# The last expert's rows: added on chip and written to the output, instead of added in device memory before a final copy

## What is computed

```python
logits = xt @ wg
gates_k, idx_k = top_k(softmax(logits), 2)          # 2 of 8 experts per token
gates_k = gates_k / sum(gates_k)
disp[e, slot] = xt[token]                            # 8 x 1024 slots, 256 features
h   = relu(einsum('ecd,edh->ech', disp, w1) + b1)    # 256 -> 1024
out = einsum('ech,ehd->ecd', h, w2) + b2             # 1024 -> 256
y   = sum over the token's two experts of gate * out[expert, slot]
x   = x + tanh(g_ffn[1]) * y
```

## Time and profile before

| | us |
|---|---|
| runs shown (three) | 2085.93, 2087.16, 2091.36 |
| their median | 2087.16 |
| the profiled execution, its own time | 2089.91 |
| the profiled execution, its span | 2088.2 |
| last matmul of the program ends | 2065.36 |
| last add issued (start) | 2069.08 |
| copy to the output issued | 2072.80 |
| copy, from issue to landing | 15.0 |

### The profile page before, as it was taken

How to read it: one execution, slowest core, us unless ns; L and a number is a source line. 1 busy time by engine, 2 the same in 40 slices (tenths; PEclk the granted TensorE clock), 3 DMA queues, 4 the chain that set the end, 5 groups by cost and what they waited for, 6 DMA issues and landing times. The chain is left out here.

```text
span 2088.2 us, 29804 instructions
## 1 busy us (share of the span) xinstructions
PE 1779.8 (85%) x10491; PEld 1063.2 (51%) x10491; DVE 1070.1 (51%) x2740; ACT 888.4 (43%) x1684; POOL 605.0 (29%) x580
## 2 busy tenths in 40 slices
PE   3799898989864988737999999999954999999995
PEld 1456555555544877613344444443322666666664
DVE  4556877787745644306877777778321112121121
ACT  3366565655531222222777787766721111111110
POOL 4212211120002777622221233211132233333322
PEclk9999999999976999967999999999976999999998
DMA  3545445334224778625323432431114133333314
GB/s 114 167 121 173 151 137 169 107 121 134 75 74 117 172 164 171 114 75 164 102 67 114 132 119 77 126 110 58 42 47 132 30 78 81 81 76 76 81 20 101
DMA packets 204243, 222.84 MB, mean 107 GB/s; under 512 B 33438, under 2 KB 195231, under 8 KB 203431
## 3 DMA queue, kind: packets, MB, share of 16 engines
q1 hardware_dynamic: 176458, 177.48, 27.7%
q0 software_dynamic: 27648, 43.60, 11.1%
HBM read 155.06 MB, written 86.93 MB: 116 GB/s over the span
## 5 line engine op out<-in xcount | busy, mean ns | idle before, releaser
L889 DVE TENSOR_REDUCE nmx<-mxb 128x1 f32<-128x512 f32 (+1 forms) x896 | 521.7, 608 | 244.0 <-PE mxb L660 147.8
L747 ACT ACTIVATE pt<-stb 128x512 f32<-128x512 f32 x832 | 475.3, 598 | 280.5 <-PE stb L680 155.9
L660 PE MATMUL mxb<-kst,qst 96*128 96x512 bf16 (+4 forms) x1024 | 335.9, 350 | 36.9 <-DVE nmx L889 27.2
L677 PE MATMUL stb<-qst,kst 99*128 99x512 bf16 (+4 forms) x1024 | 327.6, 345 | 8.2 <-DMA qst<-m3T 4.3
L1569 PE MATMUL e_h_bank<-e_xT,e_w 128*128 128x512 f32 x512 | 224.7, 597 | 6.1 <-ACT e_xT L1609 5.4
L1583 PE MATMUL e_y_bank<-e_w,e_h 128*128 128x256 f32 x1024 | 227.0, 379 | 0.0
L693 PE MATMUL ob<-pt,va 128*32 128x512 f32 (+3 forms) x2048 | 220.3, 525 | 2.7 <-ACT pt L747 1.7
L1583 PEld LDWEIGHTS e_y_bank<-e_w,e_h 128*128 128x128 f32 x1024 | 193.0, 190 | 31.7 <-issue 7.2
L677 PEld LDWEIGHTS stb<-qst,kst 102*128 102x128 bf16 (+1 forms) x1024 | 99.5, 99 | 213.3 <-ACT pt L747 136.0
L1171 POOL TENSOR_TENSOR qk<-qk,parts 128x512 f32<-128x512 f32 x64 | 73.0, 1161 | 436.4 <-ACT qk L782 227.8
L1723 POOL DMA_INDIRECT x_after_l<-e_y,e_token x64 | 99.5, 1555 | 282.0 <-DVE e_y L1688 267.3
(11 more groups left out here) (242 smaller groups left out, 2514.7 us busy)
## 6 DMA issues: line engine op xcount, KB each, us to landing
qk_parts<-parts SPq DMA_DIRECT2D x16, 1536.0 KB, 6.2
qst<-qk_parts SPq DMA_DIRECT2D x384, 64.0 KB, 2.3
kst<-qk_parts SPq DMA_DIRECT2D x384, 64.0 KB, 2.3
e_w<-in_L_ffn_w SPq DMA_DIRECT2D x16, 1024.0 KB, 7.4
rows<-rows SPq DMA_DIRECT2D x15, 1060.0 KB, 8.7
crow<-in_ctx SPq DMA_DIRECT2D x16, 512.0 KB, 3.9
x_after_l<-xres SPq DMA_DIRECT2D x16, 512.0 KB, 3.3
e_gu_nat<-in_L_ffn_gate_up_proj SPq DMA_DIRECT2D x64, 128.0 KB
```

Of the source, the lines that this page charges most:

```text
L660: last = pe.matmul(out, qst[par][0:rows_used, h, qt * P:(qt + 1) * P], kst[par][0:rows_used, h, 0:nk], start=True, stop=not causal)
L677: last = pe.matmul(bank[:, to:to + S - q_from(kt)], kst[par][0:ROWS, h, kt * P:(kt + 1) * P], qst[par][0:ROWS, h, q_from(kt):S], start=Tru ...
L747: act.activation(pt[:, slot(b, u), q0:S], stb[no % N_ST][:, q0:S], ACT.Exp, scale=SCALE).then_inc(s["st_free"], 1)
L889: last = dve.tensor_reduce(nmx[:, qt, h:h + 1], got[:, at:at + k_to(qt)], AX.X, ALU.max, negate=True)
```

## The change

The last expert does not add in device memory any more. Once the adds of experts 0 to 6 have landed, two things are issued: SP copies the sum as it then stands to the output, and POOL gathers from the same sum the rows of the last expert's tokens into a new buffer `sums` (`e_sums`). DVE waits for these rows ahead of emptying the first bank of expert 7, and for that expert multiplies by the gate and adds the gathered row in one instruction (`scalar_tensor_tensor`). POOL then waits for the copy and writes each finished tile over its tokens' rows in the output, by an indirect DMA without accumulation; rows of empty slots lie past the end and are dropped. SP and POOL end by waiting for these writes.

```diff
@@ sync
             pipeline(sp, E1, first, iteration)
-            sp.wait_ge(s["added"], 16 * TILES * E1)
+            sp.wait_ge(s["added"], 16 * TILES * (E1 - 1))
             sp.dma_start(out, x[0:T, :]).then_inc(s["copied"], 16)
             sp.wait_ge(s["copied"], 16)
+            sp.wait_ge(s["written"], 16 * TILES)
@@ vector
-            def result(b, blk):
+            def result(b, blk, last=False):
...
                 if blk == 0:
                     dve.wait_ge(s["picked"], at(2, b, 2))
+                    if last:
+                        dve.wait_ge(s["sum_in"], 16 * TILES)
...
                     for i in (2 * trip, 2 * trip + 1):
-                        dve.tensor_scalar(y[par][:, i, :], y[par][:, i, :], wcol[par][:, i:i + 1], None, ALU.mult).then_inc(s["y_done"], 1)
+                        if last:
+                            dve.scalar_tensor_tensor(out=y[par][:, i, :], in0=y[par][:, i, :], scalar=wcol[par][:, i:i + 1],
+                                                     in1=sums[:, i, :], op0=ALU.mult, op1=ALU.add).then_inc(s["y_done"], 1)
+                        else:
+                            dve.tensor_scalar(y[par][:, i, :], y[par][:, i, :], wcol[par][:, i:i + 1], None, ALU.mult).then_inc(s["y_done"], 1)
@@ gpsimd
+            def gather_sums(b):
+                pool.wait_ge(s["picked"], at(2, b, 2))
+                pool.wait_ge(s["added"], 16 * TILES * (E1 - 1))
+                for i in range(TILES):
+                    pool.indirect_dma_start(sums[:, i, :], None, x, bass.IndirectOffsetOnAxis(token[b[1]][:, i:i + 1], 0),
+                                            bounds_check=T + SPARE - 1, oob_is_err=True).then_inc(s["sum_in"], 16)
+
+            def write(b):
+                pool.wait_ge(s["copied"], 16)
+                for i in range(TILES):
+                    pool.wait_ge(s["y_done"], at(TILES, b, i + 1))
+                    pool.indirect_dma_start(out, bass.IndirectOffsetOnAxis(token[b[1]][:, i:i + 1], 0), y[b[1]][:, i, :], None,
+                                            bounds_check=T - 1, oob_is_err=False).then_inc(s["written"], 16)
+
             def iteration(cur, nxt):
                 if nxt:
                     gather(nxt)
-                add(cur)
+                    add(cur)
+                else:
+                    gather_sums(cur)
+                    write(cur)
```

More of the change, by code:

```diff
@@ L1499, in experts1 @@
                  "h_full", "act_h", "dve_h", "y_full", "y_evac", "y_done", "added", "picked", "small", "ichain",
-                 "copied", "passed")
+                 "copied", "passed", "written", "sum_in")
         s = {n: ctx.enter_context(nc.semaphore(f"e1_{n}")) for n in names}
@@ L1507, in experts1 @@
         y = two("y", [P, TILES, D])
+        sums = t_("sums", [P, TILES, D])
         b1_s, b2_s = t_("b1", [P, E1, HC]), t_("b2", [P, E1, D])
@@ L1698, in iteration @@
                 hidden(cur, 1, (1, 3, 5, 7))
-                result(cur, 0)
+                result(cur, 0, not nxt)
                 if nxt:
@@ L1702, in iteration @@
                     hidden(nxt, 0, (1, 3, 5, 7))
-                result(cur, 1)
+                result(cur, 1, not nxt)
             pipeline(dve, E1, prologue, iteration)
@@ L1728, in iteration @@
                     gather(nxt)
-                add(cur)
+                    add(cur)
+                else:
+                    gather_sums(cur)
+                    write(cur)
             pipeline(pool, E1, gather, iteration)
-            pool.wait_ge(s["added"], 16 * TILES * E1)
+            pool.wait_ge(s["written"], 16 * TILES)
 def program(nc, a, out):
```

## The result

The changed kernel takes 2071.34 us (median of 7 runs, 2067.28 to 2077.46). The kernel before, over 7 runs, has a median of 2085.93. The ratio is 0.9943 with a 95% interval of [0.9927, 0.9959]: a gain of 11.9 us, between 8.6 and 15.2. The two medians themselves lie 14.6 us apart. The predicted time was 2070.6 in a range of 2068 to 2077, and faster was given 0.93. So time and direction came out as forecast, but the forecast ratio, 2070.6 / 2087.16 = 0.992, lies just outside the interval: the gain was predicted some 4.7 us too large by the ratio, and 2.0 by the medians.

A forecast was written before the change was run, and what follows sets the result against it. TensorE bounds the last stage, then a 22.8 us tail holds the 15.0 us copy alone; -15.0 + 0.07 - 0.57 - 1.1 = -16.6 us, from 2087.16 to 2070.6 us, range 2068 to 2077.

The forecast's parts named there:

- When the moved work can start: After experts 0 to 6's adds land: copy issued 2031.5, first gather 2032.3, then every 1.31 us, last landing 2044.4.
- Copy off the path, -15.0: At the kernel's end, the copy to the output no longer follows the last add: -15.0 us.
- Multiply with add, +0.07: In the tail, DVE's fused instruction takes 424 ns against 350 for the plain multiplication, counted once: +0.07 us.
- Issue of the last but one write, -0.57: In POOL's tail, the last write starts 1.27 us after the one before, in place of 1.85: -0.57 us.
- Landing of the last write, -1.1: At the tail's end, a write lands 2.6 us after issue where an add took 3.7: -1.1 us.
- the span ends 0.4 us behind that: At the kernel's end, the span closes 0.4 us after the last landing, then the copy's at 2087.8.
- The doubtful cover: In the last expert, copy and gathers share DMA engines; gathers land by 2047.8 at the latest, still in time.
- Rival A: Last expert's gathers queue behind copy packets, TensorE loses 6.5 us: 2077.1 us; chance 0.27 with milder cases.
- Its signs: In the last expert, a TensorE gap near 2051 that ends with DVE's emptying would show Rival A.
- The cover itself: Gathered rows may land as late as 2050.8 before TensorE's third trip of the last expert stands still: 6.4 us.
- Rivals B and C: B: slow copy delays the writes, 2076.8 us, chance 0.06; C: idle TensorE loses its clock, 2100.0 us, chance 0.03.

The follow-up runs named there:

- e2: The changed kernel with SP's copy to the output held back until all eight gathers have landed: 2072.08 us, ratio 0.9946 to the kernel before.
- the second profile: The changed kernel run once more without an edit: 2072.55 us, ratio 0.9937 to the kernel before.

## Why the prediction was right, and where it was off

- **When the moved work can start**: right. The copy was issued when the adds of experts 0 to 6 had landed, the first gather 0.86 us behind it (0.76 said), then one every 1.31 to 1.39.
- **Copy off the path, -15.0**: right. It lies under TensorE's last matmuls in all versions of the changed kernel, and is 15.1 to 17.5 us long there. (In e2 it is late enough to hold up the writes.)
- **Multiply with add, +0.07**: 482 ns against 350 make +0.13. Small, but the row chosen, 424, was a single instruction on other tensors.
- **Issue of the last but one write, -0.57**: 1.28 us between the two, right.
- **Landing of the last write, -1.1**: 2.3 us in place of 3.7, so -1.4.
- **"the span ends 0.4 us behind that"**: this is the step that failed. The prediction carried the 0.4 us between landing and end over from before, and took it that nothing else runs beside the copy. Measured are 5.0, of which 4.63 are POOL's DRAIN. Nothing in the sum stood for it, and no rival had it. It was in the trace of before, in line 1495's instructions, but the views that the prediction read count only busy time.

With it the tail adds up: -15.0 + 0.13 - 0.57 - 1.4 + 4.6 = -12.2, and the tails measured are 22.8 before and 10.65 after, 12.15 less. With the gap of 0.62 that leaves 11.5 in this execution, beside 11.9 by the ratio.

That the time still came out within 0.8 us of the forecast is luck in good part. The tail became 12.2 us shorter and not 16.6. The forecast took off 16.6 from a median of three runs, 2087.16, and the median of before over seven is 2085.93, 1.2 lower; and the two medians lie 14.6 us apart, 2 to 3 us more than the profiles explain, among executions that scatter by 10 us and more.

- **The doubtful cover**: the nearest row, small transfers beside weight loads, was the wrong one to take. It gave the rows' landing 16.3 us after the copy's issue (2047.8); measured are 18.1 to 19.3. The rule of the Trainium skill ("DMA: Bandwidth & Descriptors", section "Queues, rings and completion order"), by which an engine empties a packet of one queue before it turns to the next, fits the runs in kind: pieces of 64 KB let nothing land for 14.7 us and more, pieces of 4 KB let the first gather land at 8.0.
- **Rival A** had the mechanism, but its price was too high. It added the busy times of both jobs to 23.0 us and had the rows at 25.8. They do add up, but one term was misread: 80 of the 221 packets of the earlier trace rows are under 512 bytes, at 16 to a gather those of five gathers, and the other 141 are 32 or fewer to each. So a gather has 48 packets, as the new ones have. The prediction divided by 144 and so made eight gathers 10.8 us long, where 3.5 are measured. With that the sum is 2.8 + 12.1 + 3.5 = 18.4 us, beside the 18.1 to 19.3 measured. A happened, and cost 0 to 0.6 us, because the cover was 19.3.
- **Its signs**: DVE's first emptying came 18.5 to 19.7 us behind the landing of the adds, where 13.6 was forecast, and in the first profile the third trip came 20.6 us behind it in place of 20.0. In the second profile the trip wasn't late.
- **The cover itself**, 2050.8, was a little generous: in the gapped execution the rows were complete 19.3 us after the copy's issue, and DVE started 0.45 us after that, which the limit left out.
- **Rivals B and C**: issued at once, the copy landed with 10 us or more to spare. (By the rows that B used, the 4 MB copy alone is 2.2 times as fast per byte as the 1,060 KB ones, not nearly twice.) The granted clock stayed at 1.00 (2.4 GHz) until the last matmul.

## What to carry to other kernels

A long transfer at the end of a program hides more than it shows: when it is moved away, whatever else the engines do at their end comes to light, and such instructions aren't in the busy time. Look at the last block's own line, engine by engine, before carrying a tail over. An engine that issues indirect DMAs should reach its end as early as it can, with the last wait for its data left to another engine; here that took 1.5 us off the tail. And when a bulk copy is put beside small transfers that somebody waits for, the size of its pieces sets when the first of them land, and the work of both jobs on the engines is a fair estimate of when the last do; what counts is whether that stays under the cover. To price such sharing, count the packets of one transfer in the trace: a gather here had a third of those that its rows and semaphore suggested.

## What the runs showed that was not expected

- POOL's DRAIN at the end of a block takes 4 to 4.6 us once its last DMA issue is over, whether the data has been down for 15 us (3.98) or isn't yet (4.65). It was 3.98 where the last DMAs were adds and 4.63 where they were gathers and writes; why was not tried. At the ends of two earlier stages of the kernel before it took 4.14 us (line 1233) and 5.28 (line 334), and 0.31 where no indirect DMA had been issued yet.
- Gathers that were held up behind a copy land almost together once it is through: eight of them, 1 MB, within 4.3 us in the changed kernel, where they had been issued over 9.3 us.
- A copy inside device memory of 4 MB took about the same beside the gathers in pieces of 64, 4 and 1 KB: 15.2 to 17.0, 17.5 and 17.5 us. Alone it took 15.0.
